# A selective scan in fp32: the fourth of each unit's turned state tiles is scaled by ScalarE and added by a DMA that POOL issues

## The reference, cut to what matters

```
xm, z = split(h @ W_in)                        # h: 512 rows x 512, xm and z: 512 x 1024
xm = silu(conv4(xm))                           # four taps along the rows
dt, B, C = softplus(...), xm @ W_xp[...]       # dt: 512 x 1024, B and C: 512 x 16
hst = hst * exp(dt * A) + (dt * xm) * B        # 1024 channels x 16 states, row by row
y = sum over the 16 states of hst * C          # the sum the change is about
y = (y + xm * D) * silu(z);  out = x + gate * (y @ W_out)
```

## Time and profile before

| | us |
|---|---|
| median of 3 runs (lowest, highest) | 3577.18 (3575.43, 3577.82) |
| the profiled execution (its span) | 3578.0 |
| VectorE, POOL, ScalarE busy | 2649.0, 1602.0, 1451.0 |
| first scan of the second layer, end of turn 7's additions | 1361.7, 3509.0 |

### The profile page before, as it was taken

One profiled execution on the slowest core, in us unless ns is written; L12 is line 12 of the kernel. 1 busy time (PEld: TensorE's weight loads), 2 busy tenths in 40 slices (PEclk: granted clock), 3 DMA queues, 4 the chain that ended last, 5 costly groups with the idle time before them and its releaser, 6 DMA issues.

```text
span 3578.0 us, 36146 instructions
## 1 busy us (share of the span) xinstructions
PE 2949.5 (82%) x11066; PEld 1633.8 (46%) x11066; DVE 2649.0 (74%) x3437; ACT 1451.0 (41%) x2000; POOL 1602.0 (45%) x539
## 2 busy tenths in 40 slices
PE   7999999999999985777887886886886876887765
PEld 3545455454554433345444444444444444444442
DVE  3444444444443428999999999999999999999993
ACT  1212122221221224564564564564564465565340
POOL 0121111211112105576586586587477477477671
PEclk9999999999999986977977977977977988978877
DMA  5002011020110230101131141141141131131132
GB/s 186 2 23 77 12 64 57 20 76 17 60 62 20 102 96 29 46 21 39 58 96 39 48 107 37 51 104 39 51 104 40 45 101 48 45 100 52 44 94 60
DMA packets 161658, 211.64 MB, mean 59 GB/s; under 512 B 13294, under 2 KB 78962, under 8 KB 161483
## 3 DMA queue, kind: packets, MB, share of 16 engines
q1 hardware_dynamic: 146152, 183.53, 15.9%
q0 software_dynamic: 11776, 25.17, 3.9%
q10 hardware_dynamic: 3554, 0.88, 0.1%
HBM read 167.32 MB, written 42.22 MB: 59 GB/s over the span
## 4 chain that ended last, share of the span: by engine, by line
DVE 33%; issue 14%; PE 12%; ACT 2%; DVEq 1%; POOL 1%; DMA 0%; POOLq 0%; ACTq 0%
DVE hs L1559 18%; DVE acc L1586 11%; PE bank L1165 4%; PE bank L1148 3%; PE bank L1124 2%; DVE xm L1527 2%; PE bank L1184 1%; DVEq L97 1%; PE bank L1154 1%; DVE raw L246 0%; DVE fin L1603 0%; ACT bank L1343 0%; DVE zs L1592 0%; PE bank L1172 0%; ACT acc L1333 0%
## 5 line engine op out<-in xcount | busy, mean ns | idle before, releaser
L1448 POOL TENSOR_TENSOR hs<-u,b_wide 128x2048 f32<-128x2048 f32 x256 | 1169.2, 4571 | 766.8 <-PE bank L1165 615.1
L1559 DVE TENSOR_TENSOR_SCAN hs<-bank,hs 128x512 f32<-128x512 f32 x1024 | 1243.2, 1214 | 8.5 <-issue 6.5
L1343 ACT ACTIVATE bank<-dt,decay 128x512 f32<-128x512 f32 x1024 | 699.3, 690 | 964.0 <-DVE hs L1559 960.9
L1165 PE MATMUL bank<-ident,hs 128*128 128x128 f32 x4096 | 776.8, 328 | 379.4 <-DVE hs L1559 261.2
L1165 PEld LDWEIGHTS bank<-ident,hs 128*128 128x128 f32 x4096 | 580.2, 168 | 950.6 <-issue 473.0
L1586 DVE SCALAR_TENSOR_TENSOR acc<-bank,c_t,acc 128x512 f32<-128x512 f32 x1024 | 747.5, 730 | 59.0 <-PE bank L1165 54.5
L1124 PE MATMUL bank<-h_t,w_in 128*128 128x512 f32 x1024 | 556.4, 631 | 34.3 <-ACT h_t L1274 32.9
L1184 PE MATMUL bank<-w_y,zs 128*128 128x512 f32 x512 | 275.4, 630 | 10.1 <-DVE fin L1603 5.9
L1124 PEld LDWEIGHTS bank<-h_t,w_in 128*128 128x128 f32 x1024 | 180.4, 204 | 130.7 <-issue 120.6
L558 PE MATMUL bank<-z_t,w_k 128*128 128x512 f32 x512 | 221.8, 594 | 5.9 <-ACT z_t L655 5.9
L558 PE MATMUL bank<-w_out,h_t 128*128 128x512 f32 x512 | 221.1, 592 | 0.0
(11 more groups left out here) (150 smaller groups left out, 2983.0 us busy)
## 6 DMA issues: line engine op xcount, KB each, us to landing
w_in<-in_L_cond_W_in SPq DMA_DIRECT2D x128, 256.0 KB, 3.0
b_wide<-b_rows SPq DMA_DIRECT2D x128, 256.0 KB
z<-in_x SPq DMA_DIRECT2D x8, 2048.0 KB, 8.2
res<-in_x SPq DMA_DIRECT2D x8, 2048.0 KB, 8.3
x_rows<-res SPq DMA_DIRECT2D x7, 2048.0 KB, 7.4
fin<-x_rows SPq DMA_DIRECT2D x56, 256.0 KB, 2.9
out<-fin SPq DMA_DIRECT2D x56, 256.0 KB
y_rows<-fin SPq DMA_DIRECT2D x32, 256.0 KB, 3.0
```

Of the source, the lines that this page charges most:

```text
L1165: last = nc.tensor.transpose(state_banks[n % len(state_banks)][:, j * P:(j + 1) * P], hs[:, q % RING, j, t * P:(t + 1) * P], ident[:, :])
L1343: nc.scalar.activation(decay_bank(k)[:, :], dt[:, par, j, :], ACT.Exp, scale=g.decay[:, j, s:s + 1]).then_inc(da_ready, 1)
L1448: nc.gpsimd.tensor_tensor(hs[:, q % RING, :, :], u[:, 4 * half:4 * half + 4, :], b_wide[:, s % 2, :].unsqueeze(1).to_broadcast([P, 4, CHUNK]),
L1559: nc.vector.tensor_tensor_scan(block, decay_bank(k)[:, :], block, 0.0, ALU.mult, ALU.add).then_inc(scanned, 1)
```

## The change

Of the four turned tiles of a unit, t = 0, 1 and 2 are added by VectorE as before. For t = 3, ScalarE multiplies the tile in PSUM with its column of C and writes it to one of two new places `scaled` in SBUF (`scale_state`), and POOL issues a DMA of 128x512 that adds it to `acc` (`pool_state`). The semaphores `summed` now count three additions a unit, `state_scaled` the scalings and `state_pooled[0]` and `[1]` the landed DMAs of even and of odd units. A scaling waits for the landing of the DMA two units earlier, as does the next DMA into the same half of `acc`. The turned sums wait for all of them. The path for two chunks (`both_chunks`) is not taken with these inputs and keeps its functions.

```diff
+SCALED_RING = 2
+DVE_TILES = CT - 1
+        scaled = sb("scaled", [P, SCALED_RING, 512])
...
+            def states_turned_apart(it, q, t):
+                n = CT * q + t
+                if t == 0:
+                    need(pe, scanned, BLOCKS * it + 4 * (q + 1))
+                if t == 0:
+                    need(pe, summed, DVE_TILES * (HALVES * it + q))
+                elif t == 1:
+                    need(pe, state_scaled, HALVES * it + q)
+                else:
+                    need(pe, summed, DVE_TILES * (HALVES * it + q) + t - 1)
...
+            def y_turned_apart(it, place, j):
+                need(pe, summed, DVE_TILES * HALVES * (it + 1))
+                for i in range(2):
+                    need(pe, state_pooled[i], DMA * HALVES // 2 * (it + 1))
...
+            def scale_state(it, par, q):
+                s, t = q // 2, CT - 1
+                need(act, turned, CT * HALVES * it + CT * q + t + 1)
+                need(act, state_pooled[q % 2], DMA * (HALVES // 2 * it + q // 2))
+                nc.scalar.activation(scaled[:, q % SCALED_RING, :], state_banks[(CT * q + t) % len(state_banks)][:, :], ACT.Copy,
+                                     scale=c_t[:, par, t, s:s + 1]).then_inc(state_scaled, 1)
...
+                    if n >= CT and n % CT == CT - 2:
+                        scale_state(b, par, n // CT - 1)
...
+            def pool_state(it, q):
+                t, jg = CT - 1, q % 2
+                part = acc[:, t, jg * 512:(jg + 1) * 512]
+                apart(pool, state_scaled, HALVES * it + q + 1)
+                apart(pool, state_pooled[jg], DMA * (HALVES // 2 * it + q // 2))
+                nc.gpsimd.dma_start(part, scaled[:, q % SCALED_RING, :], accum_op=ALU.add).then_inc(state_pooled[jg], DMA)
...
             def turn(b, par, prev, more):
                 for q in range(HALVES):
+                    if q >= RING:
+                        pool_state(b, q - RING)
+                    elif prev:
+                        pool_state(b - 1, HALVES - RING + q)
                     inputs(b, q)
...
-                        if q:
-                            add_states(b, par, place, q - 1, t)
+                        if q and t < DVE_TILES:
+                            add_states_apart(b, par, place, q - 1, t)
...
-                for t in range(CT):
-                    add_states(b, par, place, HALVES - 1, t)
+                for t in range(DVE_TILES):
+                    add_states_apart(b, par, place, HALVES - 1, t)
```

More of the change, by code:

```diff
@@ L869, in layer1 @@
         da_ready, inputs_ready, scanned, turned, summed, carried = (sem(n) for n in ("da_ready", "inputs_ready", "scanned", "turned1", "summed", "carried"))
+        state_scaled, state_pooled = sem("state_scaled"), [sem(f"state_pooled{i}") for i in range(2)]
         passed = sem("passed1")
@@ L1166, in states_turned @@
                 last.then_inc(turned, 1)
+            def states_turned_apart(it, q, t):
[8 more added lines that the diff above has]
+                    need(pe, summed, DVE_TILES * (HALVES * it + q) + t - 1)
+                for j in range(4):
+                    last = nc.tensor.transpose(state_banks[n % len(state_banks)][:, j * P:(j + 1) * P], hs[:, q % RING, j, t * P:(t + 1) * P], ident[:, :])
+                last.then_inc(turned, 1)
+            def y_turned_apart(it, place, j):
+                need(pe, summed, DVE_TILES * HALVES * (it + 1))
+                for i in range(2):
+                    need(pe, state_pooled[i], DMA * HALVES // 2 * (it + 1))
+                out = claimed(pe, place, "y", j)
+                for t in range(CT):
+                    last = nc.tensor.transpose(out[:, t * P:(t + 1) * P], acc[:, t, j * P:(j + 1) * P], ident[:, :])
+                last.then_inc(fills(place, "y", j), 1)
             def y_turned(it, place, j):
@@ L1191, in swap_sums @@
                     if prev:
-                        y_turned(b - 1, place, j)
+                        y_turned_apart(b - 1, place, j)
                     x_turned(place, j)
@@ L1198, in turn @@
                     for t in range(CT):
-                        states_turned(b, q, t)
+                        states_turned_apart(b, q, t)
                         if q == 0:
@@ L1235, in end @@
                     for j in range(KI):
-                        y_turned(BATCH - 1, end_place, j)
+                        y_turned_apart(BATCH - 1, end_place, j)
                     for t in range(CT):
@@ L1379, in turn @@
                         silu_z(place, n // 121)
+                scale_state(b, par, HALVES - 1)
             def front(it, par, place):
@@ L1486, in end @@
                 def end():
+                    for q in range(HALVES - RING, HALVES):
+                        pool_state(BATCH - 1, q)
                     y_complete(BATCH)
@@ L1586, in add_states, with add_states_apart @@
                 nc.vector.scalar_tensor_tensor(part, state_banks[(CT * q + t) % len(state_banks)][:, :], c_t[:, par, t, s:s + 1], part, ALU.mult, ALU.add).then_inc(summed, 1)
+            def add_states_apart(it, par, place, q, t):
+                s, jg = q // 2, q % 2
+                if q < 2:
+                    for j in (4 * jg + 2, 4 * jg + 3):
+                        need(dve, *read_by(place, "init", j))
+                else:
+                    need(dve, summed, DVE_TILES * (HALVES * it + q - 2) + t + 1)
+                need(dve, turned, CT * HALVES * it + CT * q + t + 1)
+                part = acc[:, t, jg * 512:(jg + 1) * 512]
+                nc.vector.scalar_tensor_tensor(part, state_banks[(CT * q + t) % len(state_banks)][:, :], c_t[:, par, t, s:s + 1], part, ALU.mult, ALU.add).then_inc(summed, 1)
             def gate_y(it, place, j):
```

## The result

| | us |
|---|---|
| before, median of 4 runs beside it | 3576.3 (3575.4 to 3577.8) |
| changed, median of 4 runs | 3589.8 (3586.2 to 3592.0) |
| ratio, 95% interval | 1.0032 (1.0018 to 1.0046) |
| profiled execution, span | 3590.1, before 3578.0 |

The changed kernel is slower by 13.5 us. The forecast was slower by 69 us. The sign was right and the size five times too large. The wide range (3560 to 3705) held the time; the range of the leading case alone (3600 to 3695) lies above it.

What follows compares the result with a forecast made beforehand. VectorE bounds the kernel, POOL 8% behind in each turn's last third and deciding. Turns 1 to 6 +75.6, turn 0 +4.6, turn 7 -11.2: +69 us on 3578.0, 3647, as median 3646 us; range 3560 to 3705.

Steps and rivals of the forecast that it cites:

- the leading case: Whole kernel: POOL and the end of turn bound it, 3646 us, own range 3600 to 3695, chance 0.62.
- The forecast turn end: Turn 3, VectorE's scan of unit 20 to its next first gate: 116.5 us, 22.4 more than before.
- D: Time one DMA issue holds POOL: 1.4 us with its waits, ends 0.95 and 1.86; 0.1 us of it is 9 us.
- TensorE's share: Units 1 to 19 of a turn: TensorE lets 0.8 of VectorE's 12.2 us saving through, 9.8 us; bounds 6 and 12.2.
- POOL shows idle time in units 24 to 31: Sign against the forecast, which left POOL none of its idle time late in a turn.
- Break-even: Hold of one POOL issue at which the changed kernel would be as fast as before: 0.63 us.
- The wait at the gate: First gate of a turn waits some 20 us for the turned sums; under 10 us would show the forecast wrong.
- The cheap issue: Rival: POOL's issue holds it under 0.63 us; at 0.3 us the kernel takes 3545 us, faster; chance 0.16.
- The rule that the prediction draws: POOL's issues: descriptor generation is small and variable, so one issue's hold would be near nothing; the prediction went against it.
- Late landing: Rival: the accumulating DMA lands 9 us after issue in place of 4.9, at eight turn ends; 3680 us, chance 0.08.
- TensorE at 1.2 GHz behind the longer wait: Rival: after the turn-end wait TensorE's 8 slots of new sums take longer, 7 us a turn; 3695 us, chance 0.10.
- S: With two places for scaled tiles a late landing also holds ScalarE, 1 to 2 us a turn: 3690 us.

Runs made afterwards that it cites:

- e5_two_issues: Changed kernel with a second accumulating DMA of the same size issued by POOL behind each of the 256, into an unread spare tile; 3705.4 us, ratio 1.0367.
- e6_plain: Changed kernel with its 256 DMAs copying in place of accumulating, the fourth tile's sum over states left out; 3553.3 us, ratio 0.9939.
- e1_no_dma: Changed kernel without its 256 accumulating DMAs and the waits for them, ScalarE still scaling each fourth tile; 3448.0 us, ratio 0.9656.

## Why the prediction was right or wrong

**What bounds, and who takes over: right.** POOL's 82.5 of 90 us in the last third was the number that decided. It is 88.0 now, and the gates wait 8 times for the last DMA. The forecast turn end (116.5 us from the scan of unit 20) was met with 110.9, and its parts can be laid side by side:

| term, turn 3 | forecast | measured |
|---|---|---|
| unit 19's DMA may go out, after the scan of unit 20 | 8.0 | 8.5 |
| work to the end of product 2 without issues | 86.1 | 86.1 (taken over; 86.4 by the slope of e5_two_issues) |
| 12 issues | 16.8 | 11.25 |
| last issue and landing | 4.7 | 3.95 |
| transposes and semaphores | 0.9 | 1.15 |

**The term that was mis-sized: D, the hold of one issue.** I took 1.4 us; it is 0.94. The step that failed is "the new one accumulates like the second, and reads no index. I take D = 1.4": I leaned to the row of the accumulating gather (1.56) and took nearly all of it over to a DMA without an index. As the gather's own price that row was right: in the earlier trace rows the product behind one starts 1.01 us after it and is 0.57 us longer than its kind, together 1.58. What was wrong was the step to the other kind of DMA. Accumulation, which I took for what they share, is 0.32 us of the hold (e6_plain); the 0.64 us between 1.58 and 0.94 belong to what differs, the indices or the source outside SBUF, and no run separates these two. That the lower bound, the plain gather's 0.96, is close to 0.94 looks like chance: that is a DMA with indices and without accumulation. By the forecast's own slope of 90 us for 1 us of D, 0.46 us are 41 of the 56 us by which I was too high.

**TensorE's share: off by the rest.** I let 0.8 of the saving through before unit 20. It was all of it, 12.3 us a turn (12.2 was the bound I had named), which is 17 us over seven turns. The two corrections alone turn 69 into 11 us; 13.5 were measured and 12.1 in the profile. TensorE or ScalarE does take a share, but in the last third (e1_no_dma), where POOL hides it.

**The corrected total fits better than its parts, which is luck.** With both corrections turn 0 would give 14.4 - 5.5 - 12.2 = -3.3 us, and it gave +1.6. I had POOL without idle time there, but at 0.94 us a unit without a gather-addition takes POOL 5.5 us and VectorE 6.4. Between the DMAs of units 19 and 31 of that turn POOL waits 5.5 us for scalings, as here before product 28:

```profile
1567.66 0.88 POOL L1507 DMA_DIRECT2D acc<-scaled  x1 [1.97 <-ACT scaled L1379]
```

"POOL shows idle time in units 24 to 31" was one of my signs of being wrong, and for turn 0 it came true. The other way, I counted turn 6 like turns 1 to 5, but turn 7 gathers no rows, so the stretch of issues takes 91.6 us there in place of 97.4. Turn 7 gave 2 us less than forecast, and the first scan came 3.0 us earlier. These misses nearly cancel.

**Break-even.** I put it at D = 0.63. With TensorE's share corrected it is 69 - 17 = 52 us at D = 1.4, so 0.82 us, and the plain copy at 0.62 us is faster than before in e6_plain, the accumulating one at 0.94 slower. The two runs lie on the two sides of it, though some 10 us of the distance between them are landing.

**The wait at the gate** was forecast at some 20 us and is 14.6 at the end of turn 3, 9.6 (under the 10 that I had called a sign of being wrong) to 14.7 at those of turns 0 to 6; VectorE's waits for products around unit 28 to 31 are there once, with 2.8 us in turn 3, so "a few us" was right.

**Rivals.** The cheap issue (0.16) did not happen, though its reason, that the next product starts over the issue, is real: it does, and pays it back. The rule that the prediction draws from the Trainium skill, "DMA: Bandwidth & Descriptors", section "Anatomy of one DMA — SWDGE (gpsimd) path", calls descriptor generation small and variable. The trace does not agree: 0.94 us of POOL for each DMA of 256 KB is not small beside 4.2 us to landing. Late landing: the median is 4.2 us against 4.9 for the accumulating gathers, so it is wrong. TensorE at 1.2 GHz behind the longer wait: its clock fell from 0.73 to 0.67 in the last 90 us, and the first turned sum took 1.11 us for its four transposes, but the third took 0.60 again; there I find no part of the loss. What the clock does elsewhere, ahead of unit 20, the kernel before has as well (e1_no_dma). S, late scalings, was with me only a small addition to a late landing (1 to 2 us a turn) and deserved a test of its own; it fell.

## What to carry to other kernels

An engine that only issues DMAs for others still pays for them: before work is moved to it, take its busy share in the stretch where it is fullest, not over the span, and price an issue over a long busy stretch, since neighbouring rows overlap. Then look where the last of the moved pieces stands in its list: here the order of four DMAs was worth 71 us, and leaving the last four or eight of 32 units as they were turned +13 us against the kernel before into -104 or -118.

## What the runs showed of the hardware that I had not expected

- A DMA that POOL issues overlaps in the trace with the POOL instruction behind it: that one starts 0.60 us after it and is longer by the rest. The whole hold for 128x512 fp32 inside SBUF is 0.94 us with accumulation and 0.62 us without, over twelve issues in a stretch in which POOL waits for nobody. The rows themselves have medians of 0.88 and 0.57 us, near to it; their mean (1.12 us with accumulation) is too high as a price, since a row that begins behind another issue also holds the rest of that one.
- Such an accumulating DMA lands 4.2 us after its issue in the median (3.3 to 6.5), the plain one 3.2 us (2.2 to 6.2), both sooner than the accumulating gather `fin<-y_rows` (4.9).
- The steadily busier POOL did not slow VectorE: its scans took 1.21 us and its additions 0.73 us in the mean in all of these kernels.
- TensorE's granted clock and VectorE's waits for its tiles go together before unit 20: full clock and no wait in 20 turns, 0.61 to 0.73 and 1.9 to 2.9 us of waits in 40 of the turns 1 to 6 of the ten traces.
